# FAVOR+ attention and FFN on 8 cores: squared norms read from PSUM, norm matmuls behind the feature matmuls, bo added in the step that uses it

## The reference, cut to what matters

```python
def favorplus_features(x, proj):
    xw = jnp.einsum('bhtd,hmd->bhtm', x, proj)
    xw = xw - jnp.max(xw, axis=-1, keepdims=True)
    x_norm_sq = jnp.sum(x * x, axis=-1, keepdims=True)
    return jnp.exp(xw) * jnp.exp(-0.5 * x_norm_sq) + EPS
...
Q = heads(Wq) / math.sqrt(dk); K = heads(Wk) / math.sqrt(dk); V = heads(Wv)
phiQ = favorplus_features(Q, proj) * inv_sqrt_m
phiK = favorplus_features(K, proj) * inv_sqrt_m
KV = jnp.einsum('bhtm,bhtd->bhmd', phiK, V);  Ksum = jnp.sum(phiK, axis=2)
num = jnp.einsum('bhtm,bhmd->bhtd', phiQ, KV)
den = jnp.einsum('bhtm,bhm->bht', phiQ, Ksum)[..., None] + EPS
attention = merge(num / den) @ Wo.T + bo
x = _layernorm(x + attention)
x = _layernorm(x + relu(x @ W1 + b1) @ W2 + b2)
```

## Time and profile before

| | us |
|---|---|
| median of 3 timed runs | 1598.71 |
| their range | 1597.85 to 1742.74 |
| the profiled execution, its time | 1598.1 |
| its span, first to last instruction of the slowest core (core 5) | 1596.6 |
| spans of the 8 cores | 1589.9 to 1596.6 |
| PE busy in that span | 1549.2 (97%) |
| DVE, ACT, POOL busy | 679.4, 729.8, 555.2 |

### The profile page before, as it was taken

The page is one execution under the profiler, slowest core; times in us unless marked ns, Lnnn a source line. Parts: engine busy times, 40 slices in busy tenths (PEclk is TensorE's granted clock), DMA queues, the critical chain, the costliest instruction groups (busy, mean ns, idle before and its releaser), DMA issues.

```text
span 1596.6 us, 28140 instructions; the slowest of 8 cores (1589.9 to 1596.6 us)
## 1 busy us (share of the span) xinstructions
PE 1549.2 (97%) x9816; PEld 722.8 (45%) x9816; DVE 679.4 (43%) x1385; ACT 729.8 (46%) x1663; POOL 555.2 (35%) x471
## 2 busy tenths in 40 slices
PE   8999999997898899999999999999999999999998
PEld 3455554553444344444444444444444444444443
DVE  4788888887774444444444444100011111111111
ACT  3577777776674555556655565343311111111111
POOL 4466666661354543444434433000021111111110
PEclk9999999999999999999999999999999999999999
DMA  9576678319996758476584757267674414433110
GB/s 182 135 123 107 105 107 131 66 34 226 209 211 126 197 130 198 123 171 160 126 199 132 146 156 188 79 141 149 126 250 159 150 61 165 165 97 128 60 53 40
DMA packets 260202, 219.95 MB, mean 138 GB/s; under 512 B 206048, under 2 KB 206560, under 8 KB 256608
## 3 DMA queue, kind: packets, MB, share of 16 engines
q1 hardware_dynamic: 249664, 185.65, 43.9%
q0 software_dynamic: 10400, 32.51, 13.9%
HBM read 137.38 MB, written 68.16 MB: 129 GB/s over the span
## 4 chain that ended last, share of the span: by engine, by line
PE 90%; SPq 2%; DVE 2%; DMA 2%; ACT 2%; issue 1%; POOL 0%; DVEq 0%; ACTq 0%; POOLq 0%
PE bk L73 53%; PE ps L73 37%; SPq L68 2%; DVE maxa L80 1%; ACT eq L74 1%; DMA wk0f<-WkT 1%; DMA eta<-eq 1%; ACT e L74 1%; DVE r L79 0%; DMA r<-x 0%; SPq L62 0%; DVE bia L79 0%; POOL r L77 0%; DVE mrg L77 0%; DVE qk L76 0%
## 5 line engine op out<-in xcount | busy, mean ns | idle before, releaser
L80 DVE TENSOR_REDUCE maxa<-ps 128x4 f32<-128x1024 f32 x256 | 311.8, 1218 | 119.5 <-PE ps L73 119.1
L74 ACT ACTIVATE eq<-ps,bia 128x256 bf16<-128x256 f32 x512 | 200.7, 477 | 218.7 <-DVE bia L79 107.1
L74 ACT ACTIVATE e<-ps,bia 128x256 bf16<-128x256 f32 x512 | 202.3, 487 | 90.0 <-DVE bia L79 85.3
L73 PE MATMUL bk<-rt,w 128*128 128x512 bf16 x1032 | 240.9, 379 | 0.0
L73 PE MATMUL ps<-rt,w 128*128 128x512 bf16 x1016 | 238.6, 381 | 0.0
L73 PE MATMUL ps<-w,ht 128*128 128x512 bf16 x1024 | 223.6, 379 | 0.0
L73 PE MATMUL bk<-w,ht 128*128 128x512 bf16 x1024 | 223.6, 379 | 0.0
L74 ACT ACTIVATE jnk<-out,nmu 128x1024 bf16<-128x1024 f32 x32 | 36.7, 1148 | 383.6 <-DVE nmu L78 383.6
L77 POOL TENSOR_TENSOR out<-rn,b2b 128x1024 f32<-128x1024 bf16 x32 | 68.2, 2135 | 361.4 <-DMA out<-out 334.4
L78 POOL TENSOR_SCALAR eq<-eq 128x1024 bf16<-128x1024 bf16 x88 | 91.8, 1043 | 243.6 <-ACT eq L74 243.4
L78 POOL TENSOR_SCALAR e<-e 128x1024 bf16<-128x1024 bf16 x128 | 133.5, 1043 | 106.3 <-ACT e L74 101.4
(11 more groups left out here) (85 smaller groups left out, 1443.9 us busy)
## 6 DMA issues: line engine op xcount, KB each, us to landing
h_d<-hts SPq DMA_DIRECT2D x112, 256.0 KB, 2.6
ht<-h_d SPq DMA_DIRECT2D x14, 2048.0 KB, 15.5
r<-x SPq DMA_DIRECT2D x32, 512.0 KB, 4.8
out<-out SPq DMA_DIRECT2D x32, 512.0 KB, 2.9
x_d<-xb SPq DMA_DIRECT2D x8, 1024.0 KB, 12.2
xb<-x_d SPq DMA_DIRECT2D x8, 1024.0 KB, 8.0
r1n_d<-r1n SPq DMA_DIRECT2D x32, 256.0 KB, 3.0
w<-W POOLq DMA_DIRECT2D x4, 2048.0 KB, 16.9
```

Source lines behind the costliest of these rows:

```text
L73: "matmul": lambda g, *a, **k: g.matmul(*a, **k),
L74: "activation": lambda g, *a, **k: g.activation(*a, **k),
L80: "reduce_max": lambda g, *a, **k: g.reduce_max(*a, **k),
```

## The change

Five edits. (1) `NEGN` and `norms_evac` are gone. The factor -0.5/64 sits in the matrix `ind`, the norms stay in PSUM bank 7, in two halves of 64 columns for even and odd tiles, and the bias instruction reads them there. (2) PE and DVE now share the bank: each chunk's norm matmuls wait for the last bias issued (`bias_done`), and each bias waits for the last norm matmuls issued (`norm_last`). (3) Norm matmuls that are due stand behind a group's feature matmuls, not ahead of them; in the first step too, where tile 1's chunks now follow with one chunk in reserve. (4) For rows from 39 on, `add_bo` stands in the step that uses them, behind that step's features of group 0 (group 2 for the second block of steps 42 and 43). (5) The four loads of the last `rt` tile are spread over the four groups of step 66.

```diff
--- before.py
+++ after.py
@@ -169,7 +169,6 @@
     EPSC = small("epsc", [128, 1], F32, 4)
     MAXA = [small(f"maxa{i}", [128, 16], F32, 64) for i in range(2)]
     BIA = [small(f"bia{i}", [128, 16], F32, 64) for i in range(2)]
-    NEGN = [small(f"negn{i}", [128, 64], F32, 256) for i in range(2)]
     DEN = small("den", [128, 16], F32, 64)
     RDEN = small("rden", [128, 16], F32, 64)
     S01 = [small(f"s01_{i}", [128, 2], F32, 8) for i in range(2)]
@@ -300,8 +299,8 @@
                              W2_h.rearrange("(c p) e -> p c e", p=128)[:, q * 8:(q + 1) * 8, :]))
 
 
-    qk_ready, sq_ready, negn_ready, ee_ready, va_ready = {}, {}, {}, {}, {}
-    norm_done = {}
+    qk_ready, sq_ready, bias_done, ee_ready, va_ready = {}, {}, [None], {}, {}
+    norm_done, norm_last = {}, [None]
     te, tm = {}, {}
     num_done = {}
     mgt_done = {}
@@ -355,25 +354,15 @@
 
     def norms(ti, c):
 
-        pe.wait(sq_ready[ti, c], ind_ready, *free[NSBANK])
+
+        pe.wait(sq_ready[ti, c], ind_ready, bias_done[0])
         sq = sq_of(ti, c)
         for su in range(4):
-            n0 = su * 16 + 4 * (c // 2) + c % 2
+            n0 = ti % 2 * 64 + su * 16 + 4 * (c // 2) + c % 2
             norm_done[ti, c] = pe.do("matmul", BK[NSBANK][:, n0:n0 + 3:2],
                                      sq[:, su * 128:(su + 1) * 128], IND[:, :],
                                      start=True, stop=True, mark=(su == 3))
-
-    def norms_evac(ti, gs=(0, 1, 2, 3)):
-
-        n = len(gs) * 4
-        dve.wait(norm_done[ti, 2 * gs[-1] + 1])
-        cols = [t.rearrange("p (s h) -> p s h", h=16)[:, :, 4 * gs[0]:4 * gs[0] + n]
-                for t in (NEGN[ti % 2][:, :], BK[NSBANK][:, 0:64])]
-        t = dve.do("tensor_scalar", out=cols[0], in0=cols[1], scalar1=-0.5 / 64.0, scalar2=None,
-                   op0=ALU.mult, mark=True)
-        for g in gs:
-            negn_ready[ti, g] = t
-        free[NSBANK] = (t,)
+        norm_last[0] = norm_done[ti, c]
 
     def e_part(s, g):
 
@@ -402,15 +391,13 @@
         r = dve.do("reduce_max", MAXA[s % 2][:, 4 * g:4 * g + 4],
                    PS[:, gb * 1024:(gb + 1) * 1024].rearrange("p (h m) -> p h m", h=4),
                    axis=AX.X, mark=True)
-        if between:
-            between()
-        if su == 0 and g == 0 and ti > 0:
-            norms_evac(ti)
-        dve.wait(r, negn_ready[ti, g])
+        (between or (lambda: run_norms(s, g - 1)))()
+        dve.wait(r, norm_done[ti, 2 * g + 1], norm_last[0])
+        n0 = ti % 2 * 64 + su * 16 + 4 * g
         b = dve.do("scalar_tensor_tensor", out=BIA[s % 2][:, 4 * g:4 * g + 4],
                    in0=MAXA[s % 2][:, 4 * g:4 * g + 4], scalar=-0.125,
-                   in1=NEGN[ti % 2][:, su * 16 + 4 * g:su * 16 + 4 * g + 4],
-                   op0=ALU.mult, op1=ALU.add, mark=True)
+                   in1=BK[NSBANK][:, n0:n0 + 4], op0=ALU.mult, op1=ALU.add, mark=True)
+        bias_done[0] = b
         act.wait(b)
         e, c0 = e_part(s, g)
         if s >= 32 and g % 2 == 0:
@@ -749,11 +736,16 @@
     def first_norms(g):
         norms(0, 2 * g)
         norms(0, 2 * g + 1)
-        norms_evac(0, (g,))
 
     sums = [(proj_chunk, 0, c) for c in range(3, 8)] + [(proj_chunk, 1, c) for c in range(8)] + \
         [(v_proj, su, gr) for gr in range(2) for su in range(4)]
     nth = [0]
+
+    first_due = []
+
+    def next_norms(keep=1):
+        while len(first_due) > keep:
+            norms(1, first_due.pop(0))
 
     def next_sum():
         f, a, c = sums.pop(0)
@@ -761,12 +753,10 @@
         if f is proj_chunk:
             turn = nth[0] % 2
             f(a, c, 4 + turn, dve if turn else act, dve if turn else pool)
-            if a == 1 and c > 1:
-                norms(1, c - 2)
+            if a == 1:
+                first_due.append(c)
         else:
             f(a, c, act if nth[0] % 3 == 0 else dve, 4 + nth[0] % 2)
-            if (c, a) in ((0, 0), (0, 1)):
-                norms(1, 6 + a)
 
     for c in range(3):
         proj_chunk(0, c, 4 + (c + 1) % 2, dve if c % 2 else act)
@@ -774,8 +764,10 @@
         for su in range(4):
             if su == 0:
                 first_norms(g)
-            features(su, g, su % 2)
+            features(su, g, su % 2, between=next_norms)
             next_sum()
+    next_sum()
+    next_norms(0)
     while sums:
         next_sum()
 
@@ -803,7 +795,6 @@
             if g % 2 == 1:
                 v_proj(s, g // 2, dve)
             kv_half(ti - 1, 2 * su + g // 2, g % 2)
-            run_norms(s, g)
 
 
     ups = {S_UP: 4, S_UP + 1: 4, 64: 12, 65: 12}
@@ -812,7 +803,7 @@
     for i in range(1, NTILE):
         for k in range(4):
             b = w_step(35 + 4 * i) + 2
-            rt_at.setdefault((b, k) if b <= LAST else (LAST, 3), []).append((i, k))
+            rt_at.setdefault((b, k) if b <= LAST else (LAST, k), []).append((i, k))
     for s in range(32, LAST + 1):
         ti, su = s // 4, s % 4
         nums = [r for r in range(32, 64) if n_step(r) == s]
@@ -837,6 +828,8 @@
             elif s < 64:
                 features(s, g, 0)
             spill_h()
+            if g % 2 == 0 and g // 2 < len(wos) and wos[g // 2] >= S_UP - 3:
+                add_bo(wos[g // 2])
             if 0 <= 4 * (s - 33) + g - 1 < 4:
                 eps_row(4 * (s - 33) + g - 1, 5)
             if s < S_UP:
@@ -879,8 +872,6 @@
                     transpose_m(nums[0])
                 if (len(lns) == 2 and g % 2 == 0) or (len(lns) == 1 and g == 0):
                     ln1(lns[g // 2])
-            if s < 64:
-                run_norms(s, g)
             if g == 1 and s < 64:
                 transpose_e(s, 0)
                 if s == 32:
@@ -894,8 +885,8 @@
             if len(lns) == 2 and g % 2 == 1:
                 spill_r1n(lns[g // 2])
             if g == 3:
-                for r in range(32, 64):
-                    if w_step(r) == s + 1 and r in x_ready:
+                for r in range(32, S_UP - 3):
+                    if w_step(r) == s + 1:
                         add_bo(r)
                 if nums:
                     transpose_m(nums[-1])
@@ -1028,8 +1019,8 @@
 def make_inputs(x_b, Wq, Wk, Wv, Wo, bo, proj, W1, b1, W2, b2):
     c = np.ascontiguousarray
     ind = np.zeros((128, 2), np.float32)
-    ind[0:64, 0] = 1.0
-    ind[64:128, 1] = 1.0
+    ind[0:64, 0] = -0.5 / 64.0
+    ind[64:128, 1] = -0.5 / 64.0
     pt = np.asarray(proj).transpose(0, 2, 1)
     order = [4 * g + h for g in range(4) for h in (0, 2, 1, 3)]
     WvT = np.asarray(Wv).T.reshape(D, H, DK)[:, order].reshape(D, D)
```

## The result

The changed kernel takes 1600.93 us in the median beside 1598.58 for the kernel before on the same chip: a ratio of 1.0019, 95% interval 1.001 to 1.0028. So it is 3 us slower (1.6 to 4.5), where I had forecast 0.5 us less; the time lies in the forecast's range, but the change went the other way. Some executions, whatever the kernel, are several per cent longer, with one die's cores at a lower granted clock (1742.74 us is one); the ratios leave these out.

The account below looks back on a forecast made before the run. PE's queue was taken as the bound. Terms -4.5 - 1.2 + 2.0 + 2.0 + 1.2 = -0.5 against the profiled 1598.1 gave 1597.6, stated as 1598 us; forecast's own range 1593 to 1603, wider range 1590 to 1606.

Parts of the forecast that it names:

- The first step: First step: PE waits for POOL's squares four times, about 1.1 us each on average; +2 us, bounds 0 and +7.
- The bias: Bias instruction on DVE: reading its norms from PSUM, no longer held by POOL, it always takes about 0.16 us.
- the row against the rule: Bias's fixed cost: the skill's rule gives an estimated 0.06 us more from PSUM; the profile row shows none, and was followed.
- Rival (d): Bias: still held by POOL with one input in PSUM, only losses left, 1603 us; chance 0.04.
- The key stage: Key stage: 5.9 us are waits or odd gaps, three quarters of them the bias's; -4.5 us, bounds 0 and -5.9.
- The norms' +0.02 a chunk: Norms behind the features: +0.02 us for each of 98 moved chunks, +2.0 us, bounds +1 and +11.
- Rival (a): Norms behind features: the switch is paid twice, 0.1 to 0.2 us a chunk, 1608 to 1618 us; chance 0.10.
- The margin of 0.1 us: Key stage: norms come 2.8 us behind the previous features, the latest bias is over at 2.73; costed at nothing.
- Rival (c): Bias goes free, the rest costs nothing: first step -3, key stage gains all 5.9; 1589 to 1591 us; chance 0.17.
- Rival (b): Norms stand in front of PE: margin too small or first step at its upper bound, +5 to +8, 1604; chance 0.15.
- From step 44 on: From 560 to 1000 us: PE's idle time, mostly from the norms' copy ahead of the bias, goes; -1.2 us (0 to -1.4).
- bo: Steps 42 and 43: later additions delay DVE by 0.4 and 0.7 to 0.8 us; +1.2 us (0 to +3).

Follow-up runs that it names:

- experiment 2: The changed kernel with tile 0's norms too behind their group's features; ratio to the kernel before 1.0013.
- experiment 9: The changed kernel with matmuls on zeros filling PE's idle time before tile 1's norms in the first step; ratio to the kernel before 1.0017.
- experiment 10: The changed kernel as it is, run again on the chip of the filled one; ratio to the kernel before 1.0019.
- experiment 5: The kernel before, with only the norms moved behind the features from step 4 on, still copied to SBUF; one execution, 1599.5 us, no ratio.
- experiment 4: The changed kernel with norms ahead of the next features again from step 4 on, still read from PSUM; ratio to the kernel before 1.0061.
- experiment 3: The changed kernel with the additions of bo back in group 3 of the step ahead of the use; ratio to the kernel before 1.0.
- experiment 6: The changed kernel with tile 0's norms behind their features and two chunks of tile 1's norms in reserve; ratio to the kernel before 0.9991.

## Why the prediction was wrong, point by point

**The first step** is the term that failed: +2 forecast, +4.6 measured (table: -0.3 + 5.7 - 0.8). The mechanism was as told: norms ahead of the projection meet squares that POOL hasn't made, and all of PE stands behind them. One size was off, and one cost was left out.
- I had "two waits in a row" share 2.1 us, so four waits of about 1.1, and took the steady case from the start. A core whose load is late comes near that: four waits of 4.5 us together on core 5 of experiment 2. But the usual core has two, of 2.08 and 1.77 us. With the clock kept, the step is 2.5 us longer than before (experiment 9: 14.4 + 26.8 + 11.2 = 52.4 against 49.9), so the waits were at most 0.5 more than my +2 (a filler matmul where PE had less to wait for adds to it).
- The rest, 1.5 us on the same chip (groups 6 to 15, 26.8 against experiment 10's 28.3), to 2.1 against the changed kernel's own profile (52.4 against 54.5), is the granted clock of 0.57 and 0.66 behind the waits. It was in no term. I had rows at full clock only, and priced an idle PE at the idle time alone. The bound of +7 did hold it.

With 4.6 in the place of 2 the sum -0.5 becomes +2.1, inside the ratio's interval of +1.6 to +4.5. This one term turns the sign; the two other misses below (-1.2 that wasn't there, and bo) add to it. The range held since all these terms are small beside it.

**One row was misread.** I spread the 17.5 us of waits for the exponentials over the first step, the key stage and the change to queries. But the row names `eq`, the query exponentials, and the first of those runs at 356.8 us; all 14 waits lie behind that. For the key exponentials `e` PE waited 2.2 us in 7 waits. No term of the sum used it, since the key stage's came from its length.

**The bias** was right, and with it the row against the rule. It lasts 157 to 161 ns, against up to 1292, with POOL as busy as before. The Trainium skill states the hold in SBUF — State Buffer, section "Who interferes with whom": a DVE instruction with two SBUF inputs contends with a GpSimd instruction that reads SBUF; one with at most one such input, outside DVE's two-port modes, doesn't. Experiment 5 (two inputs, up to 1673 ns) and the changed kernel (one, up to 161) agree. The Trainium skill's fixed cost for PSUM sources (VectorE: DVE Perf Modes, section "The TRN2 errata — SBUF-src ops pay a fixed extra latency per instruction") would have made it an estimated 0.06 us longer; it became 5 ns shorter in the median, and the measurement decides. Rival (d) is out.

**The key stage**: -4.5 for the bias and the key stage's share of the norms' place, 49 chunks by 0.02 or +1.0, make -3.5; measured -3.8. The 5.9 us were read on core 5, the longest of the eight (279.3 from features to features); it fell by 4.9, which with +1.0 for the norms is all of the 5.9. The median core, at 278.2, had only 4.9 to give, so three quarters of core 5's 5.9 came near it. The norms' +0.02 a chunk came out to the hundredth (4.88 to 4.90 a pair) in the changed kernel; experiment 5, with the place alone, shows no such cost in this stage. Rival (a), the switch paid twice, is out: norms start 0.33 behind the features and the projection 0.11 behind them. The margin of 0.1 us that I worried about held throughout this stage, whose length leaves no room for a longer pair. Rival (c) had this stage nearly right, and failed with the gain it saw in the first step. Rival (b) was nearer there, with a bound of +7, but the key stage has no wait of norms.

**From step 44 on** I took -1.2 for the copy ahead of the bias, and 28 of the moved chunks, +0.6. Measured +0.7 altogether. The chunks cost the 0.8 that experiments 4 and 5 both show between the two places; the -1.2 is not there (experiment 4 has 455.9 where the kernel before has 456.0, and PE's idle time from 560 to 1000 fell only from 1.4 to 1.0 us). I had put all idle time down to the copy.

**bo**: +1.2 forecast, +1.6 in step 43 and +0.2 in step 42. Experiment 3 takes 1.6 and 0.5 back, so bo costs 2.1, nearly twice the forecast; step 42 hides 0.3 of it behind a gain that no experiment isolates. By the trace of core 5 it went as told:

```profile
498.52 2.36 POOL L77 TENSOR_TENSOR r<-r,bob 128x1024 f32<-128x1024 f32 x1
...
500.98 0.69 DVE L79 SCALAR_TENSOR_TENSOR r<-ps,r 128x512 f32<-128x512 f32 x1 [4.11 <-POOL r L77]
...
509.88 0.43 SPq L62 DMA_DIRECT2D r<-x  x1
...
521.06 0.61 PE L73 MATMUL ps<-prj,qk 64*128 64x256 bf16 x4 [6.35 <-ACT eq L74]
```

The addition for rows 40 ends at 500.88 and DVE starts at 500.98; measured from the EPS addition ahead of it (497.40 here) DVE is 3.58 us behind, against 2.75 in the earlier trace rows: 0.83 late, where I had 0.7 to 0.8. The wait behind rows 41 grew from 5.24 to 6.35, by 1.1.

**Steps 32 to 41** had no term, and none is shown to be missing: the medians are 114.7 before, 113.3 and 113.7 in two executions of the changed kernel, and 114.5 in experiment 5, with cores over 5 us apart in each.

## What to carry to other kernels

A matmul that waits for a slow engine can cost more than its wait: here 1.5 us more for waits of 2.08 and 1.77 us. Price it with the low clock that may follow, and let such a matmul stand one item later in the queue (experiment 6) rather than at the first place where its data could be ready. Moving an operand to PSUM took the bias out of DVE's and POOL's contention, but tied PE and DVE to one bank, so the matmuls that write that bank must then stand where the reader is long done. In the key stage both edits gave 3.8 us, the place alone 0.6, and the operand alone lost 4.9 (283.1 against 278.2). Where a large wait hangs on a late load, look at what stands second: issuing it 4.9 us earlier (as measured from the features ahead of it) gave 2.0, since the addition then waited for its place in its own queue.

## What the runs showed of the hardware that I had not expected

- Waits of 2.08 and 1.77 us on PE, each with PE busy 0.2 to 0.4 us in the 2.0 to 2.7 us around it, are followed by a granted clock of 0.57 and 0.66 over the next 3.2 to 3.3 us. In the changed kernel's profile a stretch at the lower level follows 12 of 16 such waits. With 1.04 us of the wait filled by matmuls on zeros it stays at 1.00 on all eight cores. Experiment 10's core 4 kept 1.00 behind a wait of 1.27 us, and experiment 3's core 4 behind one of 3.04.
- A bank shared by PE and DVE costs through semaphores even where both instructions are short: 0.14 us from the end of the bias to the start of the norms, 0.18 us a chunk in all, nearly none of it in the list of waits. The Trainium skill's PSUM — Partial Sum Buffer, section "PSUM bank collisions raise a hardware error", wants such accesses guarded by bank and quadrant, or simply by bank, and not by address. No run here leaves the guard out; experiment 4 is its price at the wrong place, 8.7 us.
- DVE's squares (two SBUF inputs) are held by POOL just as the bias was: 0.42 us alone (50.63 in the changed kernel's first step), 1.02 beside POOL's. With the bias free, this is what I read as making DVE late there; no experiment moves these squares.
